# Delta rule's inverses in 64x64 tiles, their outer tables copied and fetched by rows

## The chip, the core and the metric

One core of a Trainium2 chip runs the whole kernel in one launch. The metric is the device time in microseconds, the median of several runs; lower is better. Inside one execution the times come from its profile, counted from the first instruction.

## The reference, cut to what matters

Input x is (8, 512, 128): eight sequences of 512 tokens. Two layers follow, each an attention part plus a feed-forward part on the normalized input. The part that the change touches first is the delta rule of layer 0, with 4 heads, keys of 128 and values of 32:

```python
def step(S, inp):
    q_t, k_t, v_t, b_t = inp
    pred = jnp.einsum('bhk,bhkv->bhv', k_t, S)
    delta = (v_t - pred) * b_t[..., None]
    S = S + k_t[..., :, None] * delta[..., None, :]
    o_t = jnp.einsum('bhk,bhkv->bhv', q_t, S)
    return (S, o_t)
```

The second part is layer 1's attention: 16 heads of width 8, queries by W_q, keys and values from a latent of 32, rotary positions, and a causal softmax over all 512 tokens. The rest of layer 0 is a two-layer window attention with 8 heads of 64; the rest of layer 1 is a mixture of 6 experts of which two are taken, and a shared expert.

## The kernel before, in words

**Streams.** The work of a batch (one sequence) is cut into steps, and the steps into six streams: f (projections of the window attention, and the head of the next batch), b (its scores, softmax, output and feed-forward), d (delta rule), m (layer 1's projections, gate and experts), a (layer 1's scores and their row maxima), c (layer 1's probabilities and values). In period p the streams f, b, d work on batch p and m, a, c on batch p - 1. For each engine a string in the table ORDER says from which stream its next step comes; each engine walks its string once a period, and the semaphores inside the steps do the rest. An engine's queue is so a fixed order: a step that waits holds up all behind it.

**Delta rule.** The 512 tokens are four chunks of 128. In a chunk the recurrence is turned into products with the inverse of a lower triangular 128x128 matrix, one for each head, I + L. `gram` makes L (VectorE, line L1376) and SP stores it in DRAM; `solve` fetches the 16x16 blocks on the diagonal and inverts them all at once by 15 rounds of multiply and sum on VectorE (L1387, L1388), and the result X goes through DRAM back to SBUF. The inverse of 128 is then built in levels that double the block: 16 to 32 (k = 1), 32 to 64 (k = 2), 64 to 128 (k = 3). X holds the inverse so far and Z its transpose (k = 0 is the transposition). At each level `inv_v` multiplies L with Z on TensorE (L816) into the bank V, and VectorE multiplies it with a mask that keeps only the places of the new blocks, with a minus sign, into Vm (L1396); `inv_zx` multiplies X with Vm (L830) and, but for the last level, Vm with X (L835), and VectorE adds the two products to Z (L1403) and X (L1408). All these products are of full 128x128 matrices, four heads each, in fp32, and the additions run over 128x512. The chunks go in pairs, (0, 1) and (2, 3): both chunks of a pair share a level. After a pair follow the sequential steps `seq_b`, `seq_p`, `seq_u`, `seq_o` of its two chunks.

**Score operands of layer 1.** To keep precision, the queries and keys are each split into three bf16 parts (`split`, `left`), so that a head's operand has 9 x 8 = 72 rows: each query part three times against the three key parts. `send` (L1733) stores the parts in parts_dram, three DMAs for queries and three for keys; `fetch` (L1720) brings them to Qst and Kst, in four groups of four heads, each with three query DMAs and one key DMA that repeat rows by a broadcast, behind one DMA that fills the rows of ones. The operands lie in the SBUF room that the delta rule used, so fetch waits until the last `seq_o` product. The scores `mS` (L906, L909) on TensorE and their maxima (L1447) on VectorE take turns.

**Names in the steps below.** `mq` with i = 1 projects keys from latT (L979), `latT` is scaled on VectorE (L1493), `rope` is L1503 and L1507, `fwo` adds to r1T (L1303), `mv` L996, `gate` L1002, `eu` L1010, `ew` L1014, `e_down` L1020, `fS` L664 and L678, `fPV` L698.

## Time and profile before

| what | us |
| --- | --- |
| runs: median of 3 (lowest, highest) | 2324.08 (2311.65, 2325.06) |
| the profiled execution | 2327.16 |
| its span, first to last instruction | 2325.1 |
| mean granted TensorE clock | 0.905 of full |

A clock of 1.00 is 2.4 GHz and 0.50 is 1.2 GHz. In the trace an fp32 matmul has two records, so a group of four heads shows as x8. A record's busy time is longer than the step from one start to the next, since matmuls overlap; their cost in a row is told by the starts.

### The profile page before, as it was taken

The page shows a single profiled execution, that of the slowest core. Times are in us where ns is not written, and L with a number is a line of the kernel's source. Part 1 is how long each engine was busy: PE and PEld are TensorE (multiplying, and loading weights), DVE is VectorE, ACT ScalarE, POOL GpSimd, SP SyncE. Part 2 cuts the span into 40 slices and gives each one's busy share as a digit, 9 for nine tenths or more (in the row PEclk, how much of TensorE's full clock was granted, in tenths as well). Part 3 has the DMA queues.
Part 4 walks back from the last instruction along what each step waited for, and adds up shares of the span by engine and source line. Part 5 has one row for each costly group of instructions (what it writes and reads, how often), then busy time and mean ns, then how long its engine had stood idle before and what let it go on. Part 6 is the DMA issues. An engine that isn't in the chain of part 4 may idle for free. (4 is left out here: it accounts for less than half of the span.)

```text
span 2325.1 us, 40799 instructions
## 1 busy us (share of the span) xinstructions
PE 1975.1 (85%) x15104; PEld 1289.9 (55%) x15104; DVE 1397.6 (60%) x3394; ACT 946.4 (41%) x2465; POOL 834.5 (36%) x823
## 2 busy tenths in 40 slices
PE   3796689798888979899898988899897988898677
PEld 1583459465665548555684557555593556654333
DVE  3544465676648665675756765675666756575442
ACT  2413342365325642265423652265414653255122
POOL 4407450544316441344505542263505442161000
PEclk9888789999899998999899998999899998999576
DMA  4200020100211011100201011100201012010100
GB/s 163 49 19 21 10 58 24 51 18 14 60 35 45 11 42 44 51 14 15 62 25 51 18 37 48 42 23 14 58 24 52 18 35 56 26 34 2 52 9 5
DMA packets 117524, 83.41 MB, mean 36 GB/s; under 512 B 41016, under 2 KB 104632, under 8 KB 117048
## 3 DMA queue, kind: packets, MB, share of 16 engines
q1 hardware_dynamic: 116720, 79.09, 11.9%
q8 instruction: 121, 1.98, 0.4%
q0 software_dynamic: 320, 1.05, 0.1%
q10 hardware_dynamic: 288, 0.67, 0.1%
q14 instruction: 75, 0.61, 0.1%
HBM read 46.84 MB, written 18.87 MB: 28 GB/s over the span
## 5 line engine op out<-in xcount | busy, mean ns | idle before, releaser
L1447 DVE TENSOR_REDUCE nmx<-bank 128x1 f32<-128x512 f32 (+3 forms) x352 | 225.0, 639 | 159.2 <-PE bank L909 157.9
L1163 ACT ACTIVATE shared<-bank 128x512 f32<-128x512 f32 (+1 forms) x384 | 202.9, 528 | 264.2 <-PE bank L931 260.7
L1636 POOL TENSOR_TENSOR soft<-soft,prec 128x512 f32<-128x512 f32 x128 | 138.3, 1088 | 413.0 <-DVE prec L1295 413.0
L1597 POOL TENSOR_TENSOR qk_rs<-qk_rs,minus_half 128x16 f32<-128x16 f32 x64 | 187.6, 2931 | 5.3
L1083 ACT ACTIVATE soft<-bank,nmax 128x128 f32<-128x128 f32 x512 | 179.8, 386 | 22.5 <-DVE nmax L1287 22.5
L621 PE MATMUL bank<-w_sb,hT 128*128 128x512 f32 x256 | 139.7, 633 | 24.8 <-DVE hT L1237 16.4
L931 PE MATMUL bank<-shared 75*128 75x384 bf16 (+3 forms) x512 | 150.1, 319 | 0.0
L1047 ACT ACTIVATE rot<-bank 128x512 f32<-128x512 f32 x128 | 77.5, 619 | 174.4 <-PE bank L621 174.4
L906 PE MATMUL bank<-b_sb 128*128 128x128 bf16 (+2 forms) x352 | 91.8, 261 | 66.0 <-DMA shared<-parts_dram 42.1
L909 PE MATMUL bank<-shared 72*128 72x256 bf16 (+3 forms) x512 | 138.8, 323 | 0.0
L930 PE MATMUL bank<-b_sb 128*128 128x128 bf16 x512 | 117.6, 230 | 23.1 <-ACT shared L1163 15.7
L906 PEld LDWEIGHTS bank<-b_sb 128*128 128x128 bf16 x352 | 34.9, 99 | 179.5 <-DVE nmx L1447 102.3
L1595 POOL TENSOR_SCALAR rs_f<-mv_f 128x4 f32<-128x4 f32 x24 | 5.6, 234 | 342.6 <-DVE mv_f L1226 342.0
L1140 ACT ACTIVATE U_sb<-bank 128x128 f32<-128x128 f32 x32 | 8.9, 277 | 293.2 <-PE bank L865 293.2
L593 PE MATMUL bank<-c_sb,soft 128*128 128x128 f32 x608 | 106.6, 307 | 18.1 <-POOL soft L1636 12.2
L1038 ACT ACTIVATE shared<-bank 128x512 f32<-128x512 f32 x128 | 74.7, 605 | 103.8 <-PE bank L593 51.7
L1083 ACT ACTIVATION_READ_ACCUMULATOR soft<-bank,nmax 128x1 f32 x512 | 115.9, 226 | 0.0
L1092 ACT ACTIVATE soft<-bank 128x512 f32<-128x512 f32 x128 | 75.9, 600 | 91.4 <-PE bank L593 90.8
L830 PE MATMUL bank<-shared 128*128 128x128 f32 x768 | 108.5, 284 | 0.0
L1396 DVE TENSOR_TENSOR shared<-bank,b_sb 128x512 f32<-128x512 f32 x96 | 66.3, 691 | 69.6 <-PE bank L816 69.6
L816 PE MATMUL bank<-shared 128*128 128x128 f32 x768 | 107.9, 291 | 0.1
L945 PE MATMUL bank<-shared,vaug 128*32 128x512 f32 (+3 forms) x1024 | 96.6, 475 | 11.5 <-ACT shared L1163 11.2
(236 smaller groups left out, 4913.5 us busy)
## 6 DMA issues: line engine op xcount, KB each, us to landing
vm<-v_f SPq DMA_DIRECT2D x112, 128.0 KB, 2.4
shared<-parts_dram SPq DMA_DIRECT2D x96, 96.0 KB
shared<-parts_dram SPq DMA_DIRECT2D x32, 288.0 KB
L_dram<-shared SPq DMA_DIRECT2D x32, 256.0 KB, 2.8
shared<-X_dram SPq DMA_DIRECT2D x32, 256.0 KB, 3.1
shared<-L_dram SPq DMA_DIRECT2D x32, 256.0 KB, 3.7
parts_dram<-parts SPq DMA_DIRECT2D x48, 128.0 KB, 2.3
w_sb<-weights SPq DMA_DIRECT2D x1, 4167.0 KB, 21.1
```

What stands on the lines that cost most here:

```text
L621: mm(place(("fq", "fk")[i], c)[:], hT[:, c * P:(c + 1) * P], W(f"wqkv{l}")[:, i * T:(i + 1) * T], start=True, stop=True).then_inc(fk_psum ...
L816: m = mm(ps[:, h * P:(h + 1) * P], Lc[:, h], Zc[:, h], start=True, stop=True)
L830: m = mm(ps[:, h * P:(h + 1) * P], Xc[:, h], Vc[:, h], start=True, stop=True)
L906: mm(ps[:, :, c * P:w], B("identb"), repeat(B("causal"), len(heads)), start=True, stop=False, skip_group_check=True)
L909: m = mm(ps[:, i], Qst[0:9 * DM, h * T + c * P:h * T + w], Kst[0:9 * DM, h * T:h * T + w], start=False, stop=True, skip_group_check=True)
L930: mm(ps[:, at:at + P], B("identb"), B("causalT"), start=w == 0, stop=False, skip_group_check=True)
L931: m = mm(ps[:, at:at + wide], Kst[0:9 * DM + 3, h * T + j * P:h * T + (j + 1) * P], Qst[0:9 * DM + 3, h * T + j * P:(h + 1) * T], start=Fa ...
L1083: a = af(v4(p_sb, 2, 4)[:, j, g], place("fS", j)[:, g * P:(g + 1) * P], ACT.Exp, bias=nmax[:, at:at + 1], accum_out=psums[:, at:at + 1])
L1163: af(v4(PTm, 2, GROUP)[:, u % 2, i, 0:n], place("mST")[:, 0:n], ACT.Exp).then_inc(mexp_done, 1)
L1447: reduce(v3(nmx[:], HM)[:, h:h + len(heads), c], v3(place("mS")[:, 0:len(heads) * (c + 1) * P], len(heads)), AX, ALU.max, negate=True).the ...
L1597: return tt(dst, dst, minus_half[:, 0:dst.shape[1]], ALU.pow)
L1636: tt(p, p, spread(prec[:, at:at + NPAIR], P), ALU.mult).then_inc(fnorm_done, 1)
```

## The change

**Inverses.** At levels 1 and 2 the new blocks lie inside the two 64x64 tiles on the diagonal. The products are now made per tile, with 64x64 weights and only the 32 columns that belong to new blocks (`half`), eight matmuls for four heads where there were four. Level 3 needs one 64x64 block a head: 64x64 weights, 64 columns, four matmuls. V, ZV and VX of a chunk share its banks (two banks at levels 1 and 2, one for each tile; even chunks use 0 and 1, odd ones 2 and 0). On VectorE a memset of half of Vm goes ahead of two masked copies of a tile each; both additions wait for the VX product and are two instructions each; level 3 is one negated copy into Vm and one copy into Z. The waits are moved to fit: `seq_p` of chunks 0 and 2 now has the wait for both inverses that `seq_u` had.

**Score operands.** parts_dram has 96 rows: 24 of queries and 72 of keys, the keys already three times over. `send` stores each key part three times (nine DMAs instead of three). `fetch` has two DMAs a group whose outer dimension is the row, 24 with three repeats, and 72; the fill of ones goes behind the first group.

**Order.** The strings of PE, ACT, DVE and POOL are new (SP's is the same). Of the table the first line of PE's string stands below; what moved is shown behind the diff.

```diff
@@ -39,17 +39,17 @@
     "PE": (
-        "ddbddfddfmmddfddmddbddbddbfbffbdddffdbbmbbmffmbdmmddfbddddbfmbddddddbdddbdmddmdbdbdddbdddddddddddbdddbdmdddbdb"
...
+        "ddbddfddfddmfmddfdmdddbbddbmfffbdbdddfmfbmbbfbffbmmbdbmbddddddbddddbddmddddmdddbdbddddddddbddddbddmdddbdmdddbd"
...
@@ -329,7 +329,7 @@
-            "qT": lambda h: h % 2, "V": lambda k, c: c % 2, "VX": lambda k, c: c % 2, "ZV": lambda k, c: 2,
+            "qT": lambda h: h % 2, "V": lambda k, c, r=0: ((0, 0), (0, 1), (0, 1), (1, 1))[k][r] if c % 2 == 0 else ((2, 2), (2, 0), (2, 0), (2, 2))[k][r],
...
@@ -569,6 +569,23 @@
             return 16 * (2 * (n // 2 + 1) - (n % 2) * ((n + 1) // NT))
+        def tile(ap, r):
+
+            return ap[64 * r:64 * r + 64, :, 64 * r:64 * r + 64]
+
+        def half(ap, k, upper):
+
+            return ap.rearrange("p h (m two b) -> p h m two b", two=2, b=BLK << (k - 1))[:, :, :, int(upper)]
+
+        def product(name, k, c, r):
+
+            at = ("V", "ZV", "VX").index(name) * P
+            return place("V", k, c, r)[64 * r:64 * r + 64, at:at + P].rearrange("p (h m b) -> p h m b", h=H0, b=BLK << (k - 1))
+
+        def last_product(name, c):
+            at = ("V", "ZV").index(name) * 2 * P
+            return v3(place("V", LEVELS - 1, c)[0:64, at:at + 2 * P], H0)
+
         def at_level(k, c, levels, first=0):
             return c // 2 * 2 * levels + 2 * (k - first) + c % 2
@@ -796,43 +813,53 @@
                     if k == 0:
                         pe.wait_ge(X_loaded[c % 2], 16 * (2 * b + c // 2 + 1))
-                        if c < 2:
-                            pe.wait_ge(qT_copied, H0 * b + 3 + c)
+                        if c == 0:
+                            pe.wait_ge(qT_copied, H0 * b + 3)
+                        elif c == 1:
+                            if b > 1:
+                                pe.wait_ge(fin_done, b - 1)
                         elif c == 2:
                             pe.wait_ge(Bm_done, NT * b + 2)
                         else:
-                            pe.wait_ge(o_copied, NT * b + 2)
-                        m = transposes(ps, lambda i: Xc[:, i])
+                            pe.wait_ge(S_done, (NT - 1) * b + 2)
+                        m = transposes(place("V", k, c), lambda i: Xc[:, i])
                     else:
                         if k == 1:
                             pe.wait_ge(L_loaded[c % 2], 16 * (2 * b + c // 2 + 1))
+                            if c == 0:
+                                pe.wait_ge(qT_copied, H0 * (b + 1))
+                            elif c == 2:
+                                pe.wait_ge(o_copied, NT * b + 2)
                         else:
                             pe.wait_ge(X_done, NT * (LEVELS - 2) * b + at_level(k, c, LEVELS - 2, 1) - 1)
                         pe.wait_ge(Z_done, n - 1)
                         for h in range(H0):
-                            m = mm(ps[:, h * P:(h + 1) * P], Lc[:, h], Zc[:, h], start=True, stop=True)
+                            if k == LEVELS - 1:
+                                m = mm(last_product("V", c)[:, h], Lc[64:P, h, 0:64], Zc[64:P, h, 64:P], start=True, stop=True)
+                                continue
+                            for r in range(2):
+                                m = mm(product("V", k, c, r)[:, h], tile(Lc, r)[:, h], half(tile(Zc, r), k, True)[:, h],
+                                       start=True, stop=True, skip_group_check=True)
                     m.then_inc(V_psum, 1)
                 def inv_zx(b, k, c):
-                    n = NT * LEVELS * b + at_level(k, c, LEVELS)
                     Xc, Vc = v4(X, 2, H0)[:, c % 2], v4(Vm, 2, H0)[:, c % 2]
-                    pe.wait_ge(Z_done, n)
-                    if k == 1 and c == 2:
-                        pe.wait_ge(S_done, (NT - 1) * b + 2)
-                    if k == 1 and c == 0 and b > 1:
-                        pe.wait_ge(fin_done, b - 1)
                     pe.wait_ge(Vm_done, NT * (LEVELS - 1) * b + at_level(k, c, LEVELS - 1, 1) + 1)
-                    ps = place("ZV", k, c)
                     for h in range(H0):
-                        m = mm(ps[:, h * P:(h + 1) * P], Xc[:, h], Vc[:, h], start=True, stop=True)
+                        if k == LEVELS - 1:
+                            m = mm(last_product("ZV", c)[:, h], Xc[0:64, h, 0:64], Vc[0:64, h, 64:P], start=True, stop=True)
+                            continue
+                        for r in range(2):
+                            m = mm(product("ZV", k, c, r)[:, h], tile(Xc, r)[:, h], half(tile(Vc, r), k, True)[:, h],
+                                   start=True, stop=True, skip_group_check=True)
                     m.then_inc(ZV_psum, 1)
                     if k < LEVELS - 1:
-                        ps = place("VX", k, c)
                         for h in range(H0):
-                            m = mm(ps[:, h * P:(h + 1) * P], Vc[:, h], Xc[:, h], start=True, stop=True)
+                            for r in range(2):
+                                m = mm(product("VX", k, c, r)[:, h], tile(Vc, r)[:, h], half(tile(Xc, r), k, False)[:, h],
+                                       start=True, stop=True, skip_group_check=True)
                         m.then_inc(VX_psum, 1)
                 def seq_b(b, c):
@@ -847,6 +874,8 @@
                         pe.wait_ge(o_copied, NT * b + c)
+                    if c % 2 == 0:
+                        pe.wait_ge(Z_done, NT * LEVELS * b + LEVELS * (c + 2))
@@ -857,8 +886,6 @@
                 def seq_u(b, c):
-                    if c % 2 == 0:
@@ -895,7 +922,7 @@
                     if t == 0:
-                        pe.wait_ge(group_sent[g], 4 * 16 * (b + 1))
@@ -1179,7 +1206,7 @@
                     if b and i == 0 and n == 0:
-                        act.wait_ge(parts_kept, 96 * b)
@@ -1392,20 +1419,35 @@
                     dve.wait_ge(V_psum, NT * LEVELS * b + at_level(k, c, LEVELS) + 1)
+                    Vc = v4(Vm, 2, H0)[:, c % 2]
+                    if k == LEVELS - 1:
+                        ts(Vc[0:64, :, 64:P], last_product("V", c), -1.0, None, ALU.mult).then_inc(Vm_done, 1)
+                        return
+                    nc.vector.memset(half(Vc, k, False), 0.0)
                     mask = repeat(B("lowT")[:, (k - 1) * P:k * P], H0)
-                    tt(v4(Vm, 2, H0)[:, c % 2], v3(place("V", k, c)[:], H0), mask, ALU.mult).then_inc(Vm_done, 1)
+                    for r in range(2):
+                        m = tt(half(tile(Vc, r), k, True), product("V", k, c, r), half(tile(mask, r), k, True), ALU.mult)
+                    m.then_inc(Vm_done, 1)
                 def inv_zx(b, k, c):
                     zs, xs = NT * LEVELS * b, NT * (LEVELS - 2) * b
                     Zc, Xc = v4(Z, NT, H0)[:, c], v4(X, 2, H0)[:, c % 2]
-                    dve.wait_ge(ZV_psum, NT * (LEVELS - 1) * b + at_level(k, c, LEVELS - 1, 1) + 1)
+                    if k == LEVELS - 1:
+                        dve.wait_ge(ZV_psum, NT * (LEVELS - 1) * b + at_level(k, c, LEVELS - 1, 1) + 1)
+                        nc.vector.tensor_copy(Zc[0:64, :, 64:P], last_product("ZV", c)).then_inc(Z_done, 1)
+                        return
+                    dve.wait_ge(VX_psum, xs + at_level(k, c, LEVELS - 2, 1) + 1)
                     dve.wait_ge(Z_done, zs + at_level(k - 1, c, LEVELS) + 1)
-                    tt(Zc, Zc, v3(place("ZV", k, c)[:], H0), ALU.add).then_inc(Z_done, 1)
-                    if k < LEVELS - 1:
-                        dve.wait_ge(VX_psum, xs + at_level(k, c, LEVELS - 2, 1) + 1)
-                        if k > 1:
-                            dve.wait_ge(X_done, xs + at_level(k - 1, c, LEVELS - 2, 1) + 1)
-                        tt(Xc, Xc, v3(place("VX", k, c)[:], H0), ALU.add).then_inc(X_done, 1)
+                    if k > 1:
+                        dve.wait_ge(X_done, xs + at_level(k - 1, c, LEVELS - 2, 1) + 1)
+                    for r in range(2):
+                        z = half(tile(Zc, r), k, True)
+                        m = tt(z, z, product("ZV", k, c, r), ALU.add)
+                    m.then_inc(Z_done, 1)
+                    for r in range(2):
+                        x_ = half(tile(Xc, r), k, False)
+                        m = tt(x_, x_, product("VX", k, c, r), ALU.add)
@@ -1718,28 +1760,29 @@
                 def fetch(b):
-                    sp.wait_ge(parts_kept, 96 * (b + 1))
+                    sp.wait_ge(parts_kept, 192 * (b + 1))
                     sp.wait_ge(O_psum, NT * min(b + 2, BATCH))
-                    sp.dma_start(Kst32[9 * DM:9 * DM + 3, :], row_fill).then_inc(ones_sent, 16)
                     for g in range(GROUPS):
                         at = slice(g * GROUP * T, (g + 1) * GROUP * T)
-                        for n in range(3):
-                            src = parts_dram[0][n * DM:(n + 1) * DM, at][None].to_broadcast([3, DM, GROUP * T])
-                            sp.dma_start(Qst[3 * n * DM:3 * (n + 1) * DM, at], src).then_inc(group_sent[g], 16)
-                        src = parts_dram[1][:, at][None].to_broadcast([3, 3 * DM, GROUP * T])
-                        sp.dma_start(Kst[0:9 * DM, at], src).then_inc(group_sent[g], 16)
+                        queries = parts_dram[0:3 * DM, at][:, None].to_broadcast([3 * DM, 3, GROUP * T])
+                        sp.dma_start(Qst[0:9 * DM, at], queries).then_inc(group_sent[g], 16)
+                        sp.dma_start(Kst[0:9 * DM, at], parts_dram[3 * DM:12 * DM, at]).then_inc(group_sent[g], 16)
+                        if g == 0:
+                            sp.dma_start(Kst32[9 * DM:9 * DM + 3, :], row_fill).then_inc(ones_sent, 16)
                 def send(b, i):
                     m = 2 * b + i
                     if b and i == 0:
                         for g in range(GROUPS):
-                            sp.wait_ge(group_sent[g], 4 * 16 * b)
+                            sp.wait_ge(group_sent[g], 2 * 16 * b)
                     for n in range(3):
                         sp.wait_ge(split_done, 2 * m + 1 + (n > 0))
                         sp.wait_ge(left_done, 2 * m + 1 + (n > 1))
-                        to = parts_dram[i, n * DM:(n + 1) * DM].rearrange("d (h t) -> h d t", h=HM)
-                        sp.dma_start(to, cols(parts, 3 * i + n, T)).then_inc(parts_kept, 16)
+                        for copy in range(3 if i else 1):
+                            first = 3 * DM + 3 * DM * copy + n if i else n * DM
+                            to = parts_dram[first:first + (3 * DM - 2 if i else DM):3 if i else 1]
+                            sp.dma_start(to.rearrange("d (h t) -> h d t", h=HM), cols(parts, 3 * i + n, T)).then_inc(parts_kept, 16)
@@ -1815,7 +1858,7 @@
     out = nc.dram_tensor("out", (BATCH, T, D), F32, kind="ExternalOutput").ap()
-    parts_dram = nc.dram_tensor("parts_dram", (2, 3 * DM, HM * T), BF16, kind="Internal").ap()
```

TensorE, in a middle period, around the key projections (`the,w_sb`), the window scores (`kTf,qTn`), the transposes (`c_sb,...`) and mv and gate (`w_sb,the` and 128x6). Before:

```order
L708 MATMUL bank<-oTf,w_sb 128x128 x4
L979 MATMUL bank<-the,w_sb 128x512
L593 MATMUL bank<-c_sb,q_f 128x128 x4
L593 MATMUL bank<-c_sb,k_f 128x128 x4
L979 MATMUL bank<-the,w_sb 128x512
L664 MATMUL bank<-b_sb 128x512 x2
L678 MATMUL bank<-kTf,qTn 64x128 x16
```

and now:

```order
L1006 MATMUL bank<-the,w_sb 128x512
L610 MATMUL bank<-c_sb,q_f 128x128 x4
L610 MATMUL bank<-c_sb,soft 128x128 x4
L1006 MATMUL bank<-the,w_sb 128x512
L610 MATMUL bank<-c_sb,soft 128x128 x4
...
L610 MATMUL bank<-c_sb,k_f 128x128 x4
L725 MATMUL bank<-oTf,w_sb 128x128 x4
L610 MATMUL bank<-c_sb,q_f 128x128 x4
L610 MATMUL bank<-c_sb,k_f 128x128 x4
L681 MATMUL bank<-b_sb 128x512 x2
L695 MATMUL bank<-kTf,qTn 64x128 x16
```

Both key projections, and a second pair of transposes, now stand ahead of the second `fwo` (oTf) and of the scores.

VectorE at the solve (the two memsets and the rounds that follow). Before, its end:

```order
L1387 TENSOR_TENSOR shared<-shared 128x225
L1388 TENSOR_REDUCE shared<-shared 128x15
L1493 TENSOR_SCALAR the<-bank,w_sb 32x512
L1303 TENSOR_TENSOR r1T<-bank,xnT 128x128
L1270 TENSOR_REDUCE qk_ss<-rot 128x8
```

and now, what stands ahead of its start and behind its end:

```order
L1535 TENSOR_SCALAR the<-bank,w_sb 32x512
L1403 SCALAR_TENSOR_TENSOR shared<-bank,beta,c_sb 128x128 x4
...
L1545 SCALAR_TENSOR_TENSOR acc<-bank,c_sb 128x512
L1322 RECIPROCAL prec<-psums 128x4
L1410 MEMSET shared 128x256
...
L1415 TENSOR_REDUCE shared<-shared 128x15
L1330 TENSOR_TENSOR r1T<-bank,xnT 128x128
L1545 SCALAR_TENSOR_TENSOR he<-bank,c_sb 128x512
```

latT's scaling (`the<-bank,w_sb`) and the first rope (`acc`) moved ahead of the solve; the addition to r1T stays behind it.

TensorE at the end of the second pair of chunks. Before:

```order
L816 MATMUL bank<-shared 128x128 x8
L830 MATMUL bank<-shared 128x128 x4
L708 MATMUL bank<-oTf,w_sb 128x128 x4
L830 MATMUL bank<-shared 128x128 x4
L844 MATMUL bank<-shared 128x128 x4
```

and now, the last level again:

```order
L840 MATMUL bank<-shared 64x64 x4
L725 MATMUL bank<-oTf,w_sb 128x128 x4
L840 MATMUL bank<-shared 64x64 x4
L852 MATMUL bank<-shared 64x64 x4
L1037 MATMUL bank<-xn2T,w_sb 128x512
L852 MATMUL bank<-shared 64x64 x4
L871 MATMUL bank<-shared 128x128 x4
```

An expert's projection (`xn2T,w_sb`) moved in between the last products, and a group is four small matmuls.

## Rows read from the trace of the kernel before

**Rows 1.** The page: busy time of each engine over the span.

```profile
PE 1975.1 (85%) x15104; PEld 1289.9 (55%) x15104; DVE 1397.6 (60%) x3394; ACT 946.4 (41%) x2465; POOL 834.5 (36%) x823
```

**Rows 2.** Windows: length, busy us of each engine (records), clock, DMA share, GB/s.

```profile
817.50:1083.30 265.80, 236.66 (x1888) 157.13 (x1888) 173.60 (x424) 117.69 (x309) 103.78 (x101) 0.94 0.13 35
...
0.00:285.80 285.80, 198.16 (x1392) 135.54 (x1392) 124.58 (x287) 89.89 (x250) 122.12 (x130) 0.86 0.17 53
2146.70:2325.00 178.30, 127.59 (x561) 59.41 (x558) 69.09 (x181) 38.46 (x72) 2.88 (x4) 0.64 0.06 22
```

**Rows 3.** One line (layer 0's residual, once a batch): count, ns, first and last start.

```profile
L1349 DVE TENSOR_TENSOR x_tm<-bank,x_tm x8: 691/692/692, 285.8 to 2146.7; 128x512 f32<-128x512 f32 x8
```

**Rows 4.** Waits of TensorE, 285.8 to 2146.7 us: total, times, longest.

```profile
PE bank L906 <- DMA shared<-parts_dram: 42.1, 7, 6.3
PE bank L979 <- DVE the L1493: 40.4, 7, 6.0
```

**Rows 5.** Timeline at the solve: start, length, engine, line [idle before].

```profile
858.25 0.27 DVE L1383 MEMSET shared<- 128x256 f32 x1 [0.97 <-DMA shared<-L_dram]
...
868.24 0.39 DVE L1388 TENSOR_REDUCE shared<-shared 128x15 f32<-128x225 f32 x1
869.39 2.07 PE L979 MATMUL bank<-the,w_sb 32*128 32x512 f32 x2 [5.99 <-DVE the L1493]
...
884.64 1.91 PE L816 MATMUL bank<-shared 128*128 128x128 f32 x8
```

**Rows 6.** Windows as in rows 2: after gram, and the low clock after each hole.

```profile
846.44:863.40 16.96, 15.24 (x149) 9.27 (x148) 11.15 (x39) 10.39 (x30) 9.25 (x9) 1.00 0.38 95
...
867.50:887.90 20.40, 17.82 (x86) 12.65 (x87) 9.36 (x18) 6.92 (x23) 9.00 (x8) 0.50 0.29 71
...
956.20:963.00 6.80, 4.11 (x7) 1.94 (x8) 1.29 (x2) 0.00 (x0) 1.90 (x2) 0.50 0.19 74
```

**Rows 7.** Timeline, second pair of chunks.

```profile
920.37 2.05 PE L816 MATMUL bank<-shared 128*128 128x128 f32 x16
...
923.26 0.97 PEld L835 LDWEIGHTS bank<-shared 128*128 128x128 f32 x8
923.37 1.06 PE L835 MATMUL bank<-shared 128*128 128x128 f32 x8
923.57 0.69 DVE L1403 TENSOR_TENSOR shared<-shared,bank 128x512 f32<-128x512 f32 x1 [0.42 <-PE bank L830]
...
936.76 1.06 PE L844 MATMUL bank<-shared 128*128 128x128 f32 x8
```

**Rows 8.** Timeline of TensorE: 128-wide groups, then narrow ones.

```profile
897.41 1.06 PE L830 MATMUL bank<-shared 128*128 128x128 f32 x8
898.30 1.06 PE L835 MATMUL bank<-shared 128*128 128x128 f32 x8
...
907.61 1.10 PE L678 MATMUL bank<-kTf,qTn 64*64 64x128 f32 x32
908.65 1.08 PE L865 MATMUL bank<-R_sb,shared 128*128 128x32 f32 x8
...
919.68 0.29 PE L698 MATMUL bank<-soft,v_f 128*64 128x64 f32 x4
919.80 0.29 PE L698 MATMUL bank<-soft,vm 128*64 128x64 f32 x4
```

**Rows 9.** Timeline of VectorE: eight instructions of 128x128.

```profile
843.11 2.13 DVE L1376 SCALAR_TENSOR_TENSOR shared<-bank,beta,c_sb 128x128 f32<-128x128 f32 x8
```

**Rows 10.** The fetch: timeline; DMA issues (KB each, us to landing).

```profile
948.05 0.28 SPq L1723 DMA_DIRECT2D shared<-row_fill  x1
...
950.75 0.69 SPq L1730 DMA_DIRECT2D shared<-parts_dram  x1
...
958.89 0.29 PE L906 MATMUL bank<-b_sb 128*128 128x128 bf16 x1 [5.55 <-DMA shared<-parts_dram]
...
shared<-L_dram SPq DMA_DIRECT2D x32, 256.0 KB, 3.7
```

More of the change, by code:

```diff
@@ L41 @@
     "PE": (
[L42 to L44 removed]
+        "ddbddfddfddmfmddfdmdddbbddbmfffbdbdddfmfbmbbfbffbmmbdbmbddddddbddddbddmddddmdddbdbddddddddbddddbddmdddbdmdddbd"
+        "bdbbbbbdmabamafafdamfafafamfafaffabaffmaacfacmacbacbacacbacfacfacbaccfacbacfcfacmaccmacacbacbaccabcamcafcafcca"
+        "bcfcacbacmaccacabcbcafcacbacbcabcafcacfabmcbccbcfbfccbcmcfcmccbfcbcbbbbbfcbccbcmcfcccmcbc"),
     "ACT": (
[L46 to L47 removed]
+        "ddddddffddbdddmdmbbfffbffddbddbbfffbffmmbmbmdbmbdddddddbddbdbdddddddddbmdddbddmffdffffffffbmcccbcbcfcffcbfcccf"
+        "cccbcmccbcbccffcfcbfcccfccbcccbcbcbcccbffcbcbcmcbfcfcccfccfcbcfccccfcmccb"),
     "DVE": (
[L49 to L50 removed]
+        "ddbddddfddbmfbmmmddmmmdbdfbfbmbdddbmbmbbmmmddmdddbddddddbdddbmbmdddddddddddddddddbbddmdbmbddddbbbbdamabamafafa"
+        "mafafamaafabafabbmaamaaaaaafabafabamcabbamaaaaamaaabfaabcabfabmaafaababababafmfbbcbmfbmbfbbbbbmbcmc"),
     "POOL": (
[L52 removed]
+        "dddddbbfmfffffbbffffbbbbbdffffffffffffbbffffffbbfffbbbbfffbfffffffb"),
     "SP": (
@@ L897, in mS @@
                     if t == 0:
-                        pe.wait_ge(group_sent[g], 4 * 16 * (b + 1))
+                        pe.wait_ge(group_sent[g], 2 * 16 * (b + 1))
                         if g:
@@ L1181, in split @@
                     if b and i == 0 and n == 0:
-                        act.wait_ge(parts_kept, 96 * b)
+                        act.wait_ge(parts_kept, 192 * b)
                     af(cols(parts, 3 * i + n, T), (res if n else qkf)[:], ACT.Copy).then_inc(split_done, 1)
```

11 lines of the change are left out of this document (2 added, 9 removed).

## The prediction

> **What bounds the kernel now.** I read the page first, then the windows. TensorE is busy for 85% of the span, VectorE for 60%, no other engine for over 41% [rows 1]. The batches are pipelined, so I looked for a period: one instruction that runs once a batch starts eight times from 285.8 to 2146.7 us [rows 3], 7 steps of 265.8 us. A window of such a period holds 236.7 us of matmuls and 173.6 us of VectorE, at a mean granted clock of 0.94 [rows 2]; ahead of the first lie 285.8 us, behind the last 178.3 us. So TensorE bounds a period, with 29 us idle and some work at the lower of its two clocks. The list of what it waited for in the seven periods names two holes that occur once in each: 42.1 us in 7 for the fetch of the score operands, 40.4 us in 7 for a VectorE instruction, L1493 [rows 4]; no other entry reaches 15 us.
>
> The timeline shows the second hole: the scaling of latT stands behind the 32 instructions of the 16x16 solve (858.25 to 868.5), and the projection at L979 waits for it, 6.0 us [rows 5]. The clock then stands at 0.5 (1.2 GHz) for 20.4 us, of which 17.8 are busy. The fetch's hole is followed by 6.8 us at 0.5, 4.1 of them busy [rows 6].
>
> **The inverses on TensorE.** A batch has two pairs of chunks, a pair 16 groups of four 128x128 matmuls. In the second pair they run from 920.37 to 936.76 [rows 7] with nothing else but one group at L708 of the same size: 16.39 us for 17 groups, 0.96 each, 15.4 a pair. The new groups at levels 1 and 2 are eight matmuls of 64x64 weights and 32 columns on two tiles in turn, 12 groups a pair. The trace has no such shape. Nearest rows [rows 8]: L698 (64 weight columns, 64 moving, two column tiles) starts four records, two matmuls, every 0.115 us, so 0.058 each; L678 (64x64, 128 columns, four tiles) does 16 in 1.04, 0.065 each. The moving side is no longer than theirs, so I take 0.058: 0.46 a group and 0.07 for its start (0.96 less the 0.89 from L830 to L835 in [rows 8], 0.223 a matmul), 0.53. Bounds: 0.028 a matmul (a quarter of the columns of 0.223, two at once), or 0.107 (half the weight columns, no overlap between tiles), 0.29 and 0.93 a group. Level 3 has four groups of four 64x64 matmuls with 64 columns, all on one tile: half of 0.89 and the start, 0.52; bounds 0.30 and 0.96. Sum a pair: 12 x 0.53 + 4 x 0.52 = 8.4 against 15.4, so 7.0 less, 14 a batch.
>
> For level 3 the Trainium skill ("TensorE: Matmul & The Clock Gate", Measured speedup vs the span model) says that a weight load overlaps running matmuls only if its row group differs. By that rule those groups would gain nothing, 0.96 each, and the time would be 2178. But in [rows 7] the groups of 128x128, all of one row group, show weight loads (0.97) and matmuls (1.06) side by side, so I keep 0.52. The skill's "TensorEngine Tiling" (Key Properties) says that a change of tiling mode drains the engine. With some eight changes a pair at the tail of one record, 0.17 (0.28 long, next start after 0.11), that would be 2.7 a batch and 2172. In [rows 8] L865, of the full array, starts 1.04 us after L678's first of 16 tiled ones, inside their busy time, so I charge nothing.
>
> **The inverses on VectorE.** Before, a chunk takes eight instructions of 0.69, 5.5 us. After, at levels 1 and 2 a memset of 128x256 (0.27, [rows 5]) and six of 64x128: eight of 128x128 take 2.13 [rows 9], 0.27 each, so 1.9 a level and chunk against 2.07; level 3 has two of 64x256, some 0.45 each. 4.7 against 5.5: VectorE is hardly relieved, and both additions now wait for the last product. For a pair a level was 5.8 us on TensorE; now it is 3.2 there and 3.8 on VectorE, with 0.2 to turn round: 4.0. Lead 1.5, two levels 8.0, level 3 2.0: 11.5 for a pair, against 8.4 of TensorE's own. The new order puts fPV, fwo and an expert's projection into the second pair (2.8 us), which fills most of it. I charge 2 us of new gaps a pair: gain 5, **10 a batch** (ends: 2 and 14). seq_p now waits for both chunks; seq_b's 0.9 us ahead of it cover the last copy.
>
> **The projection and latT moved.** VectorE now does latT and one rope ahead of the solve. What is late next: fS(0,2), which needs the r1T addition behind the solve. From the end of the last gram (846.44) to the hole (863.4) TensorE took 17.0 us [rows 5, 6]. The new order puts 3.1 us more between gram and fS(0,2): two projections of 0.87 (L979's one and its twin) and four groups of transposes of 0.45, less one moved ahead. So TensorE arrives 20.1 us after gram. The solve ended 22.1 us after it (868.5); the rope ahead of it adds about 1. A wait of 3 us stays. Then mv waits for the second rope, fPT for exp and POOL, and the first mask stands behind gate_pick: I put the first product at solve's end and 12 us. In equal state that is 35.5 us after gram; before it was 38.2 and 4.0 of work that is now ahead (884.64 is the start of L816, [rows 5]). Gain 6.8 at full clock; a stretch at 0.5 in it may return, mostly under waits. I take **6.5** (ends 2 and 11).
>
> **The fetch.** Before, a group was three query DMAs and one key DMA whose outer dimension is 3; the DMA share of 0.19 is 3 of 16 engines, 74 GB/s [rows 6], so 0.59 MB took some 8 us. Issued from 948.05, first used at 958.89 after 5.55 us idle, so TensorE was ready at 953.3 [rows 10]. Now two DMAs with outer 24 and 72. No row shows this; the 256 KB loads with 128 outer rows land in 3.7 us, so two, with two issues of 0.69, land in 5 to 6; at worst as before. TensorE arrives 5.3 us after the issue, and the new order adds an e_down (0.9) ahead: the wait goes. 5.6 us, and half of the 4.1 busy at 0.5: **7.5** (ends 0 and 8). Six more DMAs a batch on SP in send, at most 0.69 each by the fetch's, are hidden: SP's next step waits for the first pair. The ones row, now issued behind group 0, is needed only at the first mST.
>
> **Sum.** 10 + 6.5 + 7.5 = 24 a period, 168 in seven. The first stretch has only the inverses, less covered: 6. In the last TensorE is tied to chains with VectorE and the fetch is hidden by the experts: 0. 174 from this execution's 2327.2 gives 2153 (median of the runs 2324.1, 3 us lower; I name 2152).
>
> **Rivals.** (1) The tiles don't overlap: levels 1 and 2 gain nothing, level 3 0.44 x 8 = 3.5 a batch; 17.5 x 7 + 2 = 125 less, 2202. For it: no row has tiles (0,0) and (64,64) alone; against it: L678. (2) The waits move: VectorE has as much to do in a shorter period (170 of 242), its added small instructions make new holes, the holes at solve and fetch only shrink. 3 + 2 + 3 a period, 56 less: 2271. For it: VectorE is busy for 11.2 of the 17.0 us behind gram already [rows 6]. Against it: outside the two named holes no wait of TensorE reaches 15 us in seven periods. (3) Slower: the gaps between narrow groups bring the clock to 0.5 for the whole delta stretch (first product to last seq_o, 63 us before). It has 49 us of TensorE work left; at half clock 98, so 35 more than before, less 14 from the other two parts: 21 x 7 = 147 more, 2474. In [rows 6] the clock falls after holes of 6 us; the gaps that I expect are 1 us. It decides from 48 us of added low clock a period. (4) Nothing: under 1% either way.
>
> **Numbers.** Forecast 0.60, rival (1) 0.13, (2) 0.14, nothing 0.06, slower 0.07. A measurement tells 1% here. Faster 0.60 + 0.13 + 0.14 = 0.87. The low end has all parts near their better ends (13 + 11 + 8 a period and 10: 2090 rounded); the high end takes in rival (2), 2270.
>
> **What would show it.** A period of 242 us; groups of eight at 0.5 us and level 3 at 0.5; VectorE's 64x128 at 0.27; the two named waits under 3 and 1 us; DMA share well over 0.19 in the fetch; low clock under 20 us a period. Wrong if groups take 0.9, if new waits on masks or sums exceed 4 us a pair, or if the wait for the solve stays at 6.

## The result, and the profile after

The changed kernel takes 2294.53 us (median of 4 runs, 2277.06 to 2306.85) where the kernel before takes 2319.81 in the same comparison: a ratio of 0.989, 95% interval 0.985 to 0.993. The forecast was 2152, range 2090 to 2270. The change gains 25 us, not 168, and the time lies above the range. Where executions of one kernel fall into a faster and a slower group, the times below are those of the faster one (three of four for e2, five of ten for e8).

The windows of the changed kernel, with the columns of [rows 2]: first the seven steady periods, then the stretch ahead of them.

```profile
296.90:2125.20 1828.30, 1639.16 (x14500) 1064.34 (x14499) 1190.90 (x3150) 815.61 (x2143) 698.30 (x689) 0.90 0.15 38
...
0.00:296.90 296.90, 208.87 (x1582) 146.85 (x1583) 122.10 (x318) 90.30 (x249) 121.81 (x130) 0.76 0.16 51
```

And the same for the kernel before:

```profile
285.80:2146.70 1860.90, 1649.31 (x13154) 1094.95 (x13155) 1203.89 (x2927) 818.06 (x2143) 709.46 (x689) 0.94 0.13 35
```

A period is 261.2 us (1828.3 / 7) against 265.8, where 242 was expected. The first stretch is 11 us longer (296.9 against 285.8, [rows 2]), the last 3 us shorter (175.1). The two figures to look at are the busy time of TensorE, 1639 us against 1649 although 14 us of work a batch were to go, and the granted clock, 0.90 against 0.94. Since the clock has two levels, a mean of 0.90 says that a fifth of the time is spent at 0.50: counted over all such stretches, 52.2 us a period, against 33.6 before. In the first stretch the clock went from 0.86 to 0.76.

The waits of TensorE in the seven periods of the changed kernel, to be held against [rows 4]:

```profile
PE bank L933 <- DVE nmx L1489: 23.5, 34, 1.2
PE bank L681 <- issue: 20.6, 7, 3.0
PE bank L638 <- DVE hT L1264: 19.5, 7, 2.8
```

and one of the kernel before, over [rows 4]'s window (L906 is L933 now):

```profile
PE bank L906 <- DVE nmx L1447: 10.2, 29, 0.5
```

Both holes of [rows 4], 42.1 and 40.4 us, are gone, 11.8 us a period. In the place of one stands the wait ahead of fS (L681, 2.9 us a period), and the one for the maxima has grown from 1.5 to 3.4 a period. In all, idle time fell from 30.2 us a period ((1860.9 - 1649.3) / 7) to 27.0, where the terms of the forecast come to some 22. The larger part of what is missing is not idle time. The windows of a middle period of the changed kernel show where it is: at the solve and in the second pair of chunks.

```profile
873.80:887.50 13.70, 12.17 (x86) 9.31 (x86) 7.75 (x27) 7.04 (x24) 2.08 (x2) 0.50 0.62 163
...
914.40:918.20 3.80, 3.40 (x96) 3.14 (x96) 2.56 (x10) 0.51 (x1) 0.00 (x0) 1.00 0.00 0
918.20:942.10 23.90, 23.71 (x218) 19.72 (x218) 11.61 (x40) 1.47 (x3) 1.27 (x2) 0.50 0.01 2
```

In the kernel before, the stretch that holds the second pair is at full clock throughout:

```profile
918.20:942.10 23.90, 23.90 (x230) 22.01 (x229) 14.72 (x31) 2.74 (x6) 1.26 (x2) 1.00 0.01 2
```

The stretch at 0.50 from 918.2 has 23.7 of its 23.9 us busy, and there was no hole ahead of it: 3.4 of 3.8 us were busy. Before, the two long stretches of low clock in a period stood behind a hole of some 6 us ([rows 5, 6, 10]). The kernel before also has shorter ones without such a hole: from 993.7 to 997.1 the clock is at 0.50, and in the 7 us ahead TensorE was busy for 5.0, with no wait over 0.8. The timeline says what TensorE did before the clock fell and after (the groups at L843, L855 and L861 are the 32-column tiles):

```profile
890.05 0.66 PE L855 MATMUL bank<-shared 64*64 64x32 f32 x16
890.53 0.63 PE L861 MATMUL bank<-shared 64*64 64x32 f32 x16
891.04 0.66 PE L855 MATMUL bank<-shared 64*64 64x32 f32 x16
...
914.42 1.29 PE L843 MATMUL bank<-shared 64*64 64x32 f32 x32
...
918.39 1.06 PE L843 MATMUL bank<-shared 64*64 64x32 f32 x16 [0.31 <-DVE shared L1449]
...
922.16 1.04 PE L855 MATMUL bank<-shared 64*64 64x32 f32 x16
923.01 1.04 PE L861 MATMUL bank<-shared 64*64 64x32 f32 x16
```

In the first pair a group starts 0.49 us behind the other (890.05, 890.53, 891.04), where 0.53 was expected. In the second pair, at 0.50, the same groups take 0.85 (922.16, 923.01).

Theory A, from here: the small tiles bring the clock down themselves. Theory B: the new order does it, by gaps elsewhere. Rival C: the chain with VectorE eats the gain.

### The profile page after: what moved, and what is told of

Read it like the earlier page. It is cut to its first block and busy times, and to the rows that moved or that the text cites. A ratio compares the mean times of both kernels' runs of the same rounds, so it can differ in the third digit from the quotient of the medians.

```text
span 2300.3 us, 43957 instructions
## 1 busy us (share of the span) xinstructions
PE 1972.4 (86%) x16640; PEld 1268.8 (55%) x16640; DVE 1382.5 (60%) x3650; ACT 944.6 (41%) x2465; POOL 823.0 (36%) x823
## 5 line engine op out<-in xcount | busy, mean ns | idle before, releaser
L638 PE MATMUL bank<-w_sb,hT 128*128 128x512 f32 x256 | 146.5, 665 | 27.4 <-DVE hT L1264 21.2
L610 PE MATMUL bank<-c_sb,soft 128*128 128x128 f32 x608 | 111.0, 316 | 35.4 <-POOL soft L1678 27.3
L933 PE MATMUL bank<-b_sb 128*128 128x128 bf16 (+2 forms) x352 | 91.9, 261 | 34.2 <-DVE nmx L1489 33.3
L610 PEld LDWEIGHTS bank<-c_sb,soft 128*128 128x128 f32 x608 | 84.9, 167 | 52.4 <-POOL soft L1678 40.0
L957 PEld LDWEIGHTS bank<-b_sb 128*128 128x128 bf16 x512 | 49.8, 100 | 113.1 <-ACT shared L1190 83.3
L1297 DVE TENSOR_REDUCE qk_ss<-rot 128x8 f32<-128x512 f32 x128 | 86.5, 676 | 28.6 <-ACT rot L1074 27.7
L933 PEld LDWEIGHTS bank<-b_sb 128*128 128x128 bf16 x352 | 35.5, 101 | 118.8 <-DVE nmx L1489 92.6
L1314 DVE TENSOR_REDUCE nmax<-bank 128x4 f32<-128x512 f32 x128 | 81.8, 678 | 22.8 <-PE bank L695 22.8
```

Of the source, the lines that this page charges most:

```text
L610: m = nc.tensor.transpose(ps[0:width, i * P:(i + 1) * P], src(i), ident)
L638: mm(place(("fq", "fk")[i], c)[:], hT[:, c * P:(c + 1) * P], W(f"wqkv{l}")[:, i * T:(i + 1) * T], start=True, stop=True).then_inc(fk_psum ...
L933: mm(ps[:, :, c * P:w], B("identb"), repeat(B("causal"), len(heads)), start=True, stop=False, skip_group_check=True)
L957: mm(ps[:, at:at + P], B("identb"), B("causalT"), start=w == 0, stop=False, skip_group_check=True)
```

## Experiments 1 to 4: the forms alone, and the three parts alone

**e1.** The kernel before, with matmul forms added behind its last product. All read weights and columns from w_sb; `tiles` alternates between rows 0 to 63 and 64 to 127:

```diff
+                def tiles(n, columns, rows=(0, 1)):
+                    for i in range(n):
+                        for r in rows:
+                            at = slice(64 * r, 64 * r + 64)
+                            mm(out7[at, i % 4 * P:i % 4 * P + columns], w[at, 0:64], w[at, P:P + columns],
+                               start=True, stop=True, skip_group_check=True)
...
+                wide(230)
+                tiles(360, 32)
+                wide(230)
+                tiles(500, 64, (0,))
+                wide(230)
+                tiles(300, 64)
```

`wide(n)` is n matmuls of 128x128 weights and 128 columns. Behind the lines shown follow two tiles with 128 columns, four tiles with 128, `wide(400, 32)` (32 columns instead of 128), and 40 rounds of eight 32-column tile matmuls and four wide ones, with `wide(230)` between any two.

> The kernel before, with TensorE's forms run back to back behind its last product, each some 25 to 50 us long and behind 230 matmuls of 128x128 weights and 128 columns: 64x64 on two tiles with 32 columns, one tile with 64, two with 64, two with 128, four with 128, then 128x128 weights with 32 columns, then groups of eight 32-column tiles in turn with four wide ones. Theory A (the small tiles bring the clock down by themselves): 1.00 in the wide stretches, 0.50 in most of the stretch of two tiles with 32 columns although it is 100% busy, and at least in part of the one-tile stretch. Theory B (the clock falls only behind idle time, so in the changed kernel it is the new order's gaps): 1.00 in every stretch behind the first 4 us. Steps at full clock: 0.22 us for a wide one, 0.055 to 0.065 for a tile.

The timeline of TensorE (start, length, records):

```profile
2363.99 42.19 PE L1042 MATMUL bank<-w_sb 64*64 64x32 f32 x1440
2406.11 51.63 PE L1036 MATMUL bank<-w_sb 128*128 128x128 f32 x460
2457.67 58.54 PE L1042 MATMUL bank<-w_sb 64*64 64x64 f32 x1000
...
2567.71 35.22 PE L1042 MATMUL bank<-w_sb 64*64 64x64 f32 x1200
...
2654.41 43.88 PE L1042 MATMUL bank<-w_sb 64*64 64x128 f32 x800
```

and windows inside the stretch of 32-column tiles, that of one tile with 64 columns, that of 128x128 weights with 32 columns, and the rounds of tiles and wide ones:

```profile
2366.00:2403.00 37.00, 37.00 (x1276) 37.00 (x1272) 0.00 (x0) 0.00 (x0) 0.00 (x0) 1.00 0.02 4
2460.00:2515.00 55.00, 55.00 (x946) 55.00 (x945) 0.00 (x0) 0.00 (x0) 0.00 (x0) 1.00 0.01 2
...
2839.00:3003.00 164.00, 164.00 (x771) 164.00 (x771) 0.00 (x0) 0.00 (x0) 0.00 (x0) 0.50 0.00 1
...
3055.00:3100.00 45.00, 45.00 (x648) 40.65 (x648) 0.00 (x0) 0.00 (x0) 0.00 (x0) 1.00 0.01 2
```

Two results. Run on their own, 32-column tiles keep the full clock for 42 us: theory A in the form that was put down is wrong, for runs of that length (a longer one was not timed). In turn with wide matmuls they keep it too. But B's rule is wrong as well: 128x128 weights with 32 columns, with TensorE busy for all of 164 us, fall to 0.50. All other forms stay at 1.00. "Busy" here means that some record is running; a record lasts longer than its columns stream, so moments between the columns of short matmuls don't show as idle. And the prices: on two tiles a record takes 0.0293 us with 32 columns (42.19 / 1440) and 0.0293 with 64 (35.22 / 1200). One tile with 64 takes 0.0585, two with 128 take 0.0549. The 32 columns that the change saves are worth almost nothing to TensorE. The Trainium skill ("TensorE: Matmul & The Clock Gate", Wait — 56ns, not 53.3ns?) has a floor of about 25 ns from start to start, however few the columns; the 29 ns here agree with a floor of that kind, though the runs don't tell whether it or the loading of 64 weight columns sets the step.

**e2, e3, e4.** The kernel before with one part of the shown diff each: the inverses (with their banks and waits), send and fetch, and the strings in ORDER.

> The kernel before with the new inverses alone: old strings of steps, old send and fetch. Theory A (small tiles cost clock): low clock of 45 to 60 us in a period of 265 instead of 34, the 5 us a pair that the groups save given back, 2300 to 2330. Theory B (order's fault): inverses save their 10 us a batch, 2245 to 2260. Rival C (the chain with VectorE eats it): clock as before, 0.90, but waits of TensorE for L1426 to L1449's results grow by over 5 us a batch, 2300 to 2330 too.

> The kernel before with the new send and fetch alone. All theories: the wait for parts_dram (42 us in seven periods) goes to under 10 and the stretch of low clock behind it goes too: 7.5 us a period less, 2270 (2265 to 2285). If the time stays above 2300, the wait was only moved.

> The kernel before with the new strings of steps alone. Theory A: the wait for latT (41 us) goes, a wait before the scores takes its place at 3 us, low clock no more than before: 6.5 us a period less, 2275 (2260 to 2300). Theory B: there is a stretch at 0.50 of over 20 us in the second pair of chunks, and the time is 2300 or more.

Measured, against 2319.6: e2 2381.75 (2354.80 to 2383.35, the profiled one the fastest; ratio 1.024, 1.017 to 1.030), e3 2252.60 (0.972, 0.968 to 0.976), e4 2302.20 (0.992, 0.990 to 0.995). The seven periods of e2, in windows:

```profile
284.30:2180.30 1896.00, 1665.76 (x14499) 1081.80 (x14500) 1187.76 (x3152) 820.25 (x2143) 707.88 (x689) 0.88 0.12 34
```

of e3:

```profile
283.10:2078.50 1795.40, 1627.44 (x13154) 1083.15 (x13155) 1194.57 (x2927) 818.07 (x2143) 707.08 (x689) 0.95 0.15 39
```

and of e4:

```profile
288.10:2129.60 1841.50, 1636.13 (x13156) 1082.75 (x13155) 1201.22 (x2926) 814.14 (x2143) 698.18 (x689) 0.95 0.13 35
```

The inverses alone are slower by 62 us, in the old order. Their clock is 0.88: 66.3 us a period at 0.50, of which TensorE is busy for 59.9 (before, 26.9 of 33.6). The sum closes, with an estimate: if work at 0.50 takes twice the time, the clock costs half of what was busy at 0.50, and the rest of busy time is the work at full clock. That is 235.6 - 13.5 = 222 us a period before (1649.31 / 7 and 26.9 / 2), and 238.0 - 30.0 = 208 in e2: 14 less, as forecast. Lost again are 16.5 by the clock, and idle time grew from 30.2 to 32.9. So B is out, since the order is the old one, and C is worth some 2.7 us of idle time. The fetch gives 67 us, more than the expected range. The order gives 17, less than theory A asked for, but B's long stretch at 0.50 isn't there: the clock is 0.95, 25.4 us a period at 0.50. The order doesn't bring the clock down.

e4's waits show why it gives so little. The wait for latT is gone, but these remain, are new or have grown, and idle time fell by only 0.9 us a period:

```profile
PE bank L906 <- DMA shared<-parts_dram: 36.6, 7, 5.6
PE bank L906 <- DVE nmx L1447: 23.7, 34, 1.2
PE bank L664 <- issue: 20.6, 7, 3.0
```

## Experiments 5 to 8: all 64 columns, and the parts in pairs

What is left of theory A has two forms. A1: the clock falls where too few columns are streamed, over a mixture of small tiles, short gaps and the sequential steps (whose L892 and L908 have weights of 128x128 and 32 columns, the form that fell in e1). A2: the weights' size or the gaps alone count. Since 64 columns cost what 32 cost, they can be streamed to no purpose. e5 is the changed kernel with

```diff
             for r in range(2):
-                m = mm(product("V", k, c, r)[:, h], tile(Lc, r)[:, h], half(tile(Zc, r), k, True)[:, h],
+                m = mm(product("V", k, c, r)[:, h], tile(Lc, r)[:, h], tile(Zc, r)[:, h],
...
-            at = ("V", "ZV", "VX").index(name) * P
+            at = {"V": 0, "ZV": 0, "VX": 2 * P}[name]
```

in all three products of levels 1 and 2, with `half(...)` around `product(...)` in VectorE's reads, which take the same 32 columns out of the 64. e8 is e2 with the same edit. e6 is the change without the inverses, e7 the change without the strings.

> The changed kernel whose products of levels 1 and 2 stream all 64 columns of a tile instead of the 32 that are needed; VectorE reads the same 32. In e1 two tiles took 0.029 us a record with 32 and with 64 columns, so the groups should stay at 0.49 us at full clock. Theory A1 (the clock falls where TensorE streams too few columns a stretch): the stretch at 0.50 in the second pair of chunks (24 to 27 us) shrinks to under 10 us, low clock from 52 us a period to under 35, 2220 to 2250. Theory A2 (what counts is that only a quarter or a half of the array holds weights, or the gaps alone): no change, 2280 to 2300. If the tiles take longer with 64 columns here, 12 groups a pair by up to 0.4 us: 2320 or more.

> The change without the new inverses: new strings, new send and fetch, the groups of 128x128 as before. If the parts add up (fetch -67, order -17): 2235. If order and fetch remove the same idle time: 2250 to 2265. Theory A: low clock under 25 us a period, none in the second pair.

> The change without the new strings. If the parts add up (+62, -67): 2315. If the new order was what made room for the small tiles, more than that.

> The kernel before with the new inverses alone, as e2, but with 64 columns streamed. A1: low clock from 66 us a period to 45 or less, 2290 to 2320 instead of 2383 (what is left of the gaps between the tiles' groups still costs). A2: 2370 to 2390.

Measured: e5 2186.83 (2185.69 to 2193.45; ratio 0.944, 0.942 to 0.947), e6 2269.16 (0.979, 0.977 to 0.982), e7 2313.78 (0.996, 0.994 to 0.999), e8 2285.17 (0.985, 0.982 to 0.988). The windows of e5, its seven periods and the second pair of chunks of one of them:

```profile
269.00:2008.30 1739.30, 1550.26 (x14501) 993.06 (x14500) 1189.98 (x3151) 815.88 (x2143) 698.55 (x689) 0.95 0.15 40
...
859.10:868.40 9.30, 8.49 (x232) 7.78 (x232) 7.20 (x26) 1.16 (x2) 0.00 (x0) 1.00 0.01 4
868.40:890.00 21.60, 21.53 (x166) 14.68 (x165) 12.38 (x34) 7.51 (x14) 1.27 (x2) 1.00 0.17 49
```

and the same place in another period of the changed kernel:

```profile
1175.20:1184.40 9.20, 8.38 (x232) 7.79 (x232) 7.20 (x26) 1.15 (x2) 0.00 (x0) 1.00 0.02 4
1184.45:1211.75 27.30, 27.30 (x141) 21.46 (x140) 10.32 (x30) 3.60 (x7) 1.27 (x2) 0.50 0.00 1
```

The 9.2 us of the inverses are alike in both (232 records, 8.4 and 8.5 us busy, 7.2 of VectorE), and so is the order of what follows. Only in the one with 32 columns does the clock stand at 0.50 for the next 27.3 us. In e5 it stays at 1.00. That one edit, which adds columns that nobody reads, makes the kernel 108 us faster, more than theory A1's own figure; A2 had asked for no change. The low clock falls from 52.2 us a period to 23.4, and idle time stays at 27.0. e5 beats both kernels, and it lies inside the range of the forecast. e7 is what the parts add up to (2315); e6 is slower than either of its two sums. e8 gains 97 us on e2, as A1 says, but only 34 on the kernel before.

## Experiments 9 to 12: without idle time, and what each part is worth

**e9** replaces e1's forms by mixtures with no gaps: `tiles(pairs, tile_columns)` in turn with `wide(narrow, 32)`, that is 8, 16, 24 and 32 tile matmuls in turn with 4, 2, 1 and 1 of 128x128 weights and 32 columns.

> The kernel before, and behind its last product eight mixtures in which TensorE is never idle: pairs of two-tile 64x64 matmuls (8, 16, 24, 32 matmuls) in turn with 4, 2, 1, 1 matmuls of 128x128 weights and 32 columns, the form of the sequential steps; first with 32 columns in the tiles, then the same four with 64; 230 wide matmuls between any two. Theory A1 (columns streamed a stretch): at least one mixture reads 0.50 with 32 columns and 1.00 with 64, and none the other way round. Theory A2 (the size of the weights, or idle time only): each mixture reads the same clock with 32 and with 64.

Windows inside the eight mixtures, the four with 32 columns first (the fourth of them in two windows):

```profile
2376.00:2467.00 91.00, 91.00 (x778) 86.87 (x774) 0.00 (x0) 0.00 (x0) 0.00 (x0) 0.50 0.00 1
2526.00:2616.00 90.00, 90.00 (x1146) 85.88 (x1143) 0.00 (x0) 0.00 (x0) 0.00 (x0) 0.50 0.01 2
2683.00:2759.00 76.00, 76.00 (x1177) 73.03 (x1175) 0.00 (x0) 0.00 (x0) 0.00 (x0) 0.50 0.01 2
2814.00:2847.00 33.00, 33.00 (x944) 31.86 (x944) 0.00 (x0) 0.00 (x0) 0.00 (x0) 1.00 0.01 3
2847.00:2890.00 43.00, 43.00 (x703) 41.70 (x700) 0.00 (x0) 0.00 (x0) 0.00 (x0) 0.50 0.01 2
2944.00:3000.00 56.00, 56.00 (x837) 52.19 (x835) 0.00 (x0) 0.00 (x0) 0.00 (x0) 1.00 0.01 2
3052.00:3109.00 57.00, 57.00 (x1252) 53.21 (x1253) 0.00 (x0) 0.00 (x0) 0.00 (x0) 1.00 0.01 3
3161.00:3217.00 56.00, 56.00 (x1487) 52.73 (x1487) 0.00 (x0) 0.00 (x0) 0.00 (x0) 1.00 0.01 3
3269.00:3327.00 58.00, 58.00 (x1629) 55.27 (x1629) 0.00 (x0) 0.00 (x0) 0.00 (x0) 1.00 0.01 4
```

All four fall to 0.50 with 32 columns, the fourth, with the most tiles, only after 33 us at 1.00; all four stay at 1.00 with 64. TensorE is busy 100% of each. The size of the weights is the same on both sides, and there are no gaps between records, so A2 falls and A1 stands. What the runs don't tell apart is whether the columns themselves matter or the moments without a column inside busy records: with fewer columns there are more of these. The Trainium skill ("TensorE: Matmul & The Clock Gate", HAM oscillation — how this bites in real kernels) names idle gaps of the engine as what to avoid; here the measurement goes further than the page, since the clock falls with no idle time in the profile's rows.

**e10, e11, e12.** e10 is e7, and e12 the change without send and fetch, both with 64 columns. e11 is e3 with level 3 alone in 64x64 tiles:

```diff
+                            if k == LEVELS - 1:
+                                m = mm(v3(ps[0:64, 0:2 * P], H0)[:, h], Lc[64:P, h, 0:64], Zc[64:P, h, 64:P], start=True, stop=True)
+                                continue
                             m = mm(ps[:, h * P:(h + 1) * P], Lc[:, h], Zc[:, h], start=True, stop=True)
```

> As e7 (new inverses and fetch, old strings) but with 64 columns streamed in the tiles. If the strings are worth only what e4 and e6 showed (-17, +17): 2190 to 2205, as e5. If the new strings are what fills the gaps of the small tiles' chain (e8 kept 52 us of low clock a period): 2230 to 2260.

> As e3 (new fetch alone) with level 3 alone in 64x64 tiles, 64 columns, one tile, levels 1 and 2 in 128x128. By the prediction's 0.44 us a group on TensorE and 0.5 us a chunk on VectorE: 3.5 us a batch less on TensorE, 2225 to 2235, low clock still 24 us a period. Rival: one tile streams its 64 columns in 0.0585 us a record (e1), so four groups a pair are too short to bring the clock down, but the rule that loads of one row group do not overlap would leave it at 2252.

> As e5 (64 columns) without the new send and fetch. If the fetch is worth what e3 showed: 2187 + 67 = 2254; if as between e4 and e6: 2187 + 33 = 2220, with a wait for parts_dram of 5 us and low clock of 3 to 4 us more a period.

Measured: e10 2244.42 (ratio 0.967, 0.964 to 0.970), e11 2239.31 (0.965, 0.962 to 0.969), e12 2225.96 (0.960, 0.956 to 0.963). Together:

| inverses | old order, old fetch | old order, new fetch | new order, old fetch | new order, new fetch |
| --- | --- | --- | --- | --- |
| 128x128 | 2319.6 | 2252.6 (e3) | 2302.2 (e4) | 2269.2 (e6) |
| tiles, 32 columns | 2381.8 (e2) | 2313.8 (e7) | | 2294.5 (the change) |
| tiles, 64 columns | 2285.2 (e8) | 2244.4 (e10) | 2226.0 (e12) | 2186.8 (e5) |

Down the last column, the tiles cost 25 us with 32 columns and give 82 with 64. With the new fetch, the new order is worth 58 us where the full tiles are (e10 to e5) and costs 17 where there are none (e3 to e6); with the old fetch it gains 59 and 17. The new fetch is worth 67 us on the kernel before and 39 beside the new order and the full tiles (e12 to e5). In the old order the full tiles give 34 us with the old fetch and 8 with the new one, where level 3 alone gives 13 (e3 to e11): e10 has 31 us a period at 0.50 where e3 has 24, so there the full tiles don't hold the clock everywhere.

## Why the prediction was wrong

**The step that failed** is rival (3)'s weighing: "In [rows 6] the clock falls after holes of 6 us; the gaps that I expect are 1 us." That took holes for the only cause of a low clock. With it the forecast priced 14 us of TensorE's work a batch as 14 us of time at full clock, and put the clock's answer to the small tiles at nothing. The work left, but with 32-column tiles between the steps of 32 columns the clock falls without a hole (e5 and e9 show that the columns do it), and the time at 0.50 gave the gain back. In us a period, counted as for e2 (the forecast's idle time: 4 of new gaps, less 6.5 at the solve and 5.6 of the fetch's hole):

| | before | change forecast | change measured |
| --- | --- | --- | --- |
| work at full clock | 222.2 | -14 | -13.3 |
| lost by the clock | 13.5 | -2 | +11.8 |
| idle | 30.2 | -8 | -3.2 |
| sum | 265.8 | -24 | -4.7 |

Of the 19 us that are missing, the clock is 14 and idle time 5. Rival (3) named the effect, but its cause was gaps between the groups, it placed it in the whole stretch of the delta rule, and it gave it 0.07. The low clock grew by 19 us a period, not by the 48 from which that rival would have decided. The kernel still came out faster, by 1.1%, because the fetch's gain (67 us in e3) outweighs what the inverses cost (62 in e2).

**Inverses on TensorE.** The price of a group was right: 0.53 forecast, 0.49 measured. Level 3 was put at 0.52 and takes about 0.61, by the starts of the changed kernel's timeline:

```profile
897.51 0.68 PE L840 MATMUL bank<-shared 64*64 64x64 f32 x8 [0.26 <-DVE shared L1449]
898.12 0.60 PE L681 MATMUL bank<-b_sb 128*128 128x512 bf16 x2
```

That is 0.35 less than 0.96, 2.8 a batch in eight groups, of which e11's 13 us over eight batches show 1.7. The bound that the tiles might not overlap was off: on two tiles 64 columns go twice as fast as on one (0.0293 against 0.0585). The Trainium skill's rule ("TensorE: Matmul & The Clock Gate", The mechanism) is that a weight load overlaps a running matmul only if its row group differs; this trace doesn't agree. In e1's stretch on one tile, so in one row group, TensorE and its weight loads are each busy for 55.0 of 55.0 us. The 0.96 that the forecast drew from that rule was its own reading; 0.61 was measured. Half of 0.223 is 0.112, not the 0.107 of the upper bound, which makes the bound 0.96 a group instead of 0.93; no term rests on it. And a change between tiles and 128-wide work was charged at nothing. In e1's last rounds the groups start at

```profile
3055.36 0.66 PE L1042 MATMUL bank<-w_sb 64*64 64x32 f32 x16
3055.95 1.16 PE L1036 MATMUL bank<-w_sb 128*128 128x128 f32 x8
3057.04 0.66 PE L1042 MATMUL bank<-w_sb 64*64 64x32 f32 x16
```

so a round of 1.68 us holds 16 records at 0.0293 and 8 at 0.112, 1.37: some 0.15 us a change, as an estimate, twice the 0.07 that the forecast charged a group for its start. With 64 columns the inverses give 82 us beside order and fetch, against 76 forecast (10 a batch in seven periods, and 6).

**Inverses on VectorE.** Right: in the changed kernel's groups of instructions the memset takes 0.27 us and the 64x128 pieces 0.28 (0.29 at L1445 and L1449),

```profile
L1426 DVE MEMSET shared<- 128x256 f32 x64 | 17.4, 272 | 43.6 <-PE bank L843 39.8
L1429 DVE TENSOR_TENSOR shared<-bank,b_sb 64x128 f32<-64x128 f32 x128 | 35.4, 277 | 1.4
```

and TensorE's largest wait for them (L843 for L1449) is 7.1 us in 14 over the whole run.

**latT and the projection.** The new wait ahead of the scores was called at 3 us and is 2.9. But 6.5 us a period was too much: e4 shows 17 us in the whole kernel, 2.4 a period, near the lower end of 2. The old hole took 5.9 us a period and the new one takes 2.9, which leaves 3.0, and in e4 other waits ate most of that. The earlier first product of the inverses, on which the rest of the term stood, didn't come. In the changed kernel it is

```profile
888.49 0.66 PE L843 MATMUL bank<-shared 64*64 64x32 f32 x16
```

and the last product of gram ends at 848.6: 40 us, where 35.5 was expected. Between them lies the stretch at 0.50 behind the new hole (873.8 to 887.5), busy for 12.2 of its 13.7 us, where the forecast had it "mostly under waits".

**The fetch.** The mechanism was right and its size too small: 7.5 a period forecast with 8 as the better end, 67 us measured in e3, 9.3 a period (1795.4 / 7 is 256.5, against 265.8). 6.2 of it is idle time (the hole, 6.0), and 3.1 is busy time, which fell from 235.6 to 232.5 with the same work: the clock, which the forecast had put at 2. The first issue of the changed kernel:

```profile
948.50 0.86 SPq L1768 DMA_DIRECT2D shared<-parts_dram  x1
```

and the window that holds all of them:

```profile
948.50:955.00 6.50, 6.50 (x25) 3.06 (x26) 2.29 (x4) 4.79 (x9) 0.00 (x0) 1.00 0.58 159
```

Before, the same stretch had a DMA share of 0.15 and 61 GB/s. It is 0.58 and 159 GB/s now, and TensorE is busy through all of it; the first score product starts at 954.5, 6 us behind the issue.

**The first stretch.** It was to be 6 us shorter and is 11 longer: its work at full clock is 20 us less, but the clock costs 31 more. Most of that is one stretch of the changed kernel, in its first delta rule:

```profile
95.60:184.30 88.70, 82.90 (x815) 74.13 (x815) 31.49 (x101) 15.88 (x52) 5.38 (x6) 0.50 0.10 27
```

The kernel before has a mean clock of 0.87 in that window. In e5 the first stretch has the same instructions at a clock of 0.88 and is 28 us shorter than in the changed kernel:

```profile
0.00:269.00 269.00, 177.89 (x1582) 117.04 (x1583) 121.91 (x319) 90.52 (x249) 121.99 (x130) 0.88 0.18 57
```

**Open.** Why order and fetch together (e6) are 17 us slower than the fetch alone was not settled; a period has 1.3 us more of idle time and 1.0 more lost by the clock. e5's period is 248.5 us where 242 was expected: 27.0 of idle time where the forecast comes to some 22, and 211 of work where it comes to 208. That its total lies near the forecast is in part luck, since its first stretch is 11 us shorter than expected.

## What to carry to other kernels

Before making matmuls smaller, ask what they do to the clock and not only to the busy time: cutting columns that cost nothing (32 instead of 64 in a 64x64 tile) can halve the clock of what follows, here for 17 to 27 us in every period. A profile shows it as busy time that doesn't fall although work was removed, together with a lower granted clock; read the two side by side. Where fewer columns save no time, as here, stream the whole tile and let VectorE pick. And time the parts of a change alone: here +62, -67 and -17 us hid behind a sum of -25.

## What was unexpected of the hardware

The clock falls to 0.50 in a TensorE stream without idle time in its rows: 128x128 weights with 32 columns (164 us at 0.50, 100% busy), and each of four mixtures of it with 32-column tiles, one of them only after 33 us, while the same mixtures with 64 columns and 42 us of the 32-column tiles alone stayed at 1.00. Turns of tiles and 128-wide matmuls cost some 0.15 us a change (estimate, e1). A 64x64 fp32 record on two tiles in turn takes 0.0293 us with 32 and with 64 columns; 64x64 weights with 128 columns take 0.0549 on two tiles.
